# Attention of an adaptive-norm block in two groups of two batches, gates built on four partitions, output bias added by GpSimd

## What is computed

```python
mod = (_silu(L0_c) @ L0_wmod).reshape(L0_c.shape[0], 6, 1, -1)
sa, ca, ga, sb, cb, gb = (mod[:, 0], mod[:, 1], mod[:, 2], mod[:, 3], mod[:, 4], mod[:, 5])
ga = (2 * (ga >= 0) - 1) * jnp.maximum(jnp.abs(ga), 0.25)
gb = (2 * (gb >= 0) - 1) * jnp.maximum(jnp.abs(gb), 0.25)
h = _layernorm(x, axis=-1) * (1 + ca) + sa
x = x + ga * _L0_attn_ref(h, ...)
h = _layernorm(x, axis=-1) * (1 + cb) + sb
x = x + gb * _L0_ffn_ref(h, L0_ffn_w_gate, L0_ffn_w_up, L0_ffn_w_down)
```

## Time and profile before

| | us |
|---|---|
| median of 3 runs | 959.33 (958.27 to 960.14) |
| profiled execution | 958.83 |
| its span, first to last instruction | 957.1 |
| TensorE busy in the span | 663.8 (69%) |
| VectorE busy | 677.4 (71%) |
| GpSimd busy | 567.0 (59%) |
| ScalarE busy | 439.1 (46%) |

### The profile page before, as it was taken

One profiled execution on the slowest core, in us unless ns is written; L12 is line 12 of the kernel. 1 busy time (PEld: TensorE's weight loads), 2 busy tenths in 40 slices (PEclk: granted clock), 3 DMA queues, 4 the chain that ended last, 5 costly groups with the idle time before them and its releaser, 6 DMA issues.

```text
span 957.1 us, 8556 instructions
## 1 busy us (share of the span) xinstructions
PE 663.8 (69%) x2416; PEld 337.7 (35%) x2416; DVE 677.4 (71%) x867; ACT 439.1 (46%) x715; POOL 567.0 (59%) x297
## 2 busy tenths in 40 slices
PE   3675576567377797878788386787978744299990
PEld 2344244432032232323322032232323224288880
DVE  6742477566598889899945598999998865844430
ACT  2413142257576465555556666465565513022220
POOL 6101564400399888999900399898998913136555
PEclk9755677688589899899997589899999975599995
DMA  4000000000000000000000000000000061012222
GB/s 154 0 1 1 0 1 0 1 0 0 1 0 0 1 0 0 0 0 0 0 1 0 1 0 1 0 0 1 0 0 0 0 241 44 1 12 19 20 21 22
DMA packets 11363, 13.05 MB, mean 14 GB/s; under 512 B 1545, under 2 KB 9914, under 8 KB 10690
## 3 DMA queue, kind: packets, MB, share of 16 engines
q1 hardware_dynamic: 6434, 10.51, 3.0%
q0 software_dynamic: 4896, 2.13, 2.6%
HBM read 8.43 MB, written 4.21 MB: 13 GB/s over the span
## 4 chain that ended last, share of the span: by engine, by line
PE 33%; DVE 29%; issue 14%; POOL 10%; ACT 9%; DMA 2%; DVEq 1%; POOLq 0%; ACTq 0%; SPq 0%
PE ps L924 7%; DVE ps L1302 6%; DVE hs_all L1315 6%; POOL hc_all L456 4%; PE ps L1050 3%; PE ps L1066 3%; PE ps L1027 2%; DVE w_ffn L1315 2%; PE ps L930 2%; ACT ps L693 2%; PE ps L886 2%; PE ps L769 1%; POOL dbu L443 1%; DVE big L1117 1%; DVE dbu L1349 1%
## 5 line engine op out<-in xcount | busy, mean ns | idle before, releaser
L924 PE MATMUL ps<-hc_all,ident 128*128 128x512 f32 x512 | 264.0, 640 | 21.6 <-POOL hc_all L456 20.4
L456 POOL TENSOR_TENSOR hc_all<-hs_all,c_row 128x1024 f32<-128x1024 f32 x88 | 210.5, 2392 | 19.4 <-DVE hs_all L1315 16.2
L690 ACT COPY c_row<-ps 128x512 f32<-128x512 f32 x128 | 74.9, 585 | 161.6 <-PE ps L943 145.9
L924 PEld LDWEIGHTS ps<-hc_all,ident 128*128 128x128 f32 x512 | 100.5, 201 | 119.1 <-issue 73.6
L1315 DVE TENSOR_TENSOR_SCAN hs_all<-da,ps 128x1024 f32<-128x1024 f32 x48 | 109.8, 2287 | 11.6 <-ACT da L693 5.4
L693 ACT ACTIVATE da<-big,a_neg 128x511 f32 (+1 forms) x176 | 117.2, 716 | 0.0
L1302 DVE TENSOR_TENSOR ps<-big,ps 128x1024 f32<-128x1024 f32 x88 | 107.4, 1220 | 11.7 <-POOL big L432 4.8
L456 POOL TENSOR_TENSOR hc_all<-w_ffn,c_row 128x1024 f32<-128x1024 f32 x40 | 94.2, 2356 | 22.1 <-DVE w_ffn L1315 22.1
L1315 DVE TENSOR_TENSOR_SCAN hs_all<-ps,dbu 128x1024 f32<-128x1024 f32 x40 | 91.0, 2274 | 12.4 <-POOL hc_all L456 9.7
L443 POOL TENSOR_TENSOR dbu<-big,w_mod 128x1024 f32<-128x1024 f32 x40 | 96.1, 2401 | 0.0
L1315 DVE TENSOR_TENSOR_SCAN w_ffn<-da,ps 128x1024 f32<-128x1024 f32 x40 | 91.5, 2287 | 5.3
(11 more groups left out here) (253 smaller groups left out, 1103.3 us busy)
## 6 DMA issues: line engine op xcount, KB each, us to landing
tmpA<-w_in SPq DMA_DIRECT2D x2, 1024.0 KB, 6.9
tmpB<-w_in SPq DMA_DIRECT2D x2, 1024.0 KB, 9.0
x_tok<-x_in SPq DMA_DIRECT2D x1, 1024.0 KB, 6.6
out<-x_tok SPq DMA_DIRECT2D x1, 1024.0 KB, 7.2
xm_rows<-xn SPq DMA_DIRECT2D x1, 1024.0 KB, 5.3
w_mod<-w_mod_in SPq DMA_DIRECT2D x1, 768.0 KB, 4.6
out<-hc_all,hs_all POOLq DMA_INDIRECT x40, 3.0
w_ffn<-w_ffn_in SPq DMA_DIRECT2D x1, 560.0 KB, 7.4
```

The source lines that it names most:

```text
L456: nc.gpsimd.tensor_tensor(hc[:, n % 4, :, :], hs3[HS_BUF[n]].rearrange("p (i s) -> p i s", i=IC), c_row[:, n % 4, :].unsqueeze(1).to_broad ...
L690: nc.scalar.copy(c_row[:, n % 4, :], ps[:, CB, :]).then_inc(c_cs, 1)
L924: mm = nc.tensor.matmul(ps[:, YS + i, :], ident[:], hc[:, n % 4, i, :], start=(n == 0), stop=(n == NS - 1))
```

## The change

- Loads: x in two halves, `w_mod` by block, block 1's after `w_ffn`. The bias is loaded on 128 partitions (`bt_rows`).
- Modulation: block 0's shift and scale of the first norm stay columns (`modulation_cols`). All else is made as rows on four partitions, one per batch (`modulation_rows`: `silu_c` of four columns is the stationary side). ScalarE and VectorE make the gates there (`gate_rows`, `gate_signs`). Later a matmul with a broadcast column of the identity spreads a batch's row over 128 partitions (mod_bc). Block 1's are made after the attention.
- Attention: maxima, exps and sums in groups of two batches (`pool_max`, `key_weights`, `value_weights`). ScalarE copies the keys. The `w_ffn` rounding stands behind the key weights.
- Output: no matmul for the bias. GpSimd makes `bt_gate` and adds it to `x_tok`, four instructions of 128x512, and VectorE then adds the output of a batch and takes its statistics at once. `std` and `nmr` are made after every second batch. The transposes of `w_ffn` stand between batches 1 and 2, in banks 4 to 6.
- Some semaphores are merged, for block 1 too; its instructions and their order stay.

```diff
-            sp.dma_start(w_mod[:], w_mod_in).then_inc(ld_mod, 16)
-            sp.dma_start(x_tok[:], x_in).then_inc(ld_x, 16)
+            for k in range(2):
+                ts = slice(k * NT // 2, (k + 1) * NT // 2)
+                sp.dma_start(x_tok[:, ts, :], x_in[:, ts, :]).then_inc(ld_x[k], 16)
+                if k == 0:
+                    sp.dma_start(w_mod[:, 0, :], w_mod_in[:, 0, :]).then_inc(ld_mod[0], 16)
             sp.dma_start(w_attn[:], w_attn_in).then_inc(ld_attn, 16)
-            sp.dma_start(bt_row[:], bt_in).then_inc(ld_bt, 16)
             sp.dma_start(w_ffn[:], w_ffn_in).then_inc(ld_ffn, 16)
+            sp.dma_start(bt_rows[:], bt_in).then_inc(ld_bt, 16)
+            sp.dma_start(w_mod[:, 1, :], w_mod_in[:, 1, :]).then_inc(ld_mod[1], 16)
...
+            pool.wait_ge(ld_bt, 16)
+            pool.wait_ge(mod_done, 1)
+            chain.link(nc.gpsimd.tensor_tensor(bt_gate[:], bt_rows[:].unsqueeze(1).to_broadcast([P, B, D]), gates[:, 0, :, :],
+                                               ALU.mult))
+            for b in range(B):
+                pool.wait_ge(xn_ready, TB * (b + 1))
+                xb = x_tok[:, b * TB:(b + 1) * TB, :]
+                nc.gpsimd.tensor_tensor(xb, xb, bt_gate[:, b, :].unsqueeze(1).to_broadcast([P, TB, D]),
+                                        ALU.add).then_inc(x_bias, 1)
+            pool.wait_ge(mod_done, 2)
             modulate_x(0)
...
-            act.wait_ge(mod_raw, 3)
-            nc.scalar.activation(gate_abs, gates[:], ACT.Abs, scale=2.0).then_inc(mod_abs, 1)
...
+            def gate_rows(layer, rows, gate):
+                act.wait_ge(mod_mm, 2 + layer)
+                nc.scalar.copy(mod_rows[:, rows, :], ps[0:B, 7, 0:(4 - 2 * layer) * D].rearrange("p (j d) -> p j d", d=D))
+                nc.scalar.activation(row_abs[:, 2 * layer:2 * layer + 2, :],
...
+            def exps(k, g, at):
+                act.wait_ge(a_bias, 2 * k + g + 1)
+                for b in range(2 * g, 2 * g + 2):
+                    nc.scalar.activation(soft[:, b, :], ps[:, 4 + b, :], ACT.Exp, bias=sc4[:, at, b:b + 1], scale=SCALE,
+                                         accum_out=sc4[:, at + 1, b:b + 1]).then_inc(a_exp_s, 1)
+
...
+            keys(0)
+            keys(1)
+            exps(0, 0, 2)
+            keys(2)
+            keys(3)
+            exps(0, 1, 2)
             magnitudes(q_x, 0, w_ffn[:], q_mag[:])
...
+            act.wait_ge(mod_bc, 1)
+            nc.scalar.copy(gates[:, 0, :, :], ps[:, 0:B, 0:D]).then_inc(mod_done, 1)
+            act.wait_ge(a_pooled, B)
+            exps(1, 0, 9)
+            nc.scalar.copy(shift_b[:], ps[:, 0:B, D:2 * D])
+            nc.scalar.activation(scale_b[:], ps[:, 0:B, 2 * D:3 * D], ACT.Identity, bias=1.0)
+            nc.scalar.copy(gates[:, 1, :, :], ps[:, 0:B, 3 * D:4 * D]).then_inc(mod_done, 1)
+            exps(1, 1, 9)
...
+            def deviations(g):
+                ts = slice(g * NT // 2, (g + 1) * NT // 2)
+                act.wait_ge(stat_ready, NT + (g + 1) * NT // 2)
+                nc.scalar.activation(std[:, ts], mv[:, ts, 1], ACT.Sqrt, bias=eps[:, 0:1]).then_inc(std_ready, 1)
...
+            deviations(0)
             normalise_x(0)
             normalise_x(1)
+            deviations(1)
+            act.preload_act_table(ACT.Silu)
+            gate_rows(1, slice(4, 6), slice(0, 2))
             magnitudes(q_x, 1, x_flat(0), mag_x)
+            act.wait_ge(mod_bc, 2)
+            nc.scalar.copy(gates[:, 2:4, :, :].rearrange("p g (h k) d -> p h k g d", h=2),
+                           ps[:, 6:8, :].rearrange("p h (k g d) -> p h k g d", k=2, g=2)).then_inc(mod_done, 1)
...
-            def modulation():
-                pe.wait_ge(c_ready, 1)
-                pe.wait_ge(ld_mod, 16)
-
-                for b in range(B):
-                    nc.tensor.matmul(ps[:, b, :], silu_c[:, b:b + 1].to_broadcast([P, P]), w_mod[:, 0, 2 * D:6 * D],
-                                     start=True, stop=True).then_inc(mod_mm, 1)
-
-                for i, (layer, j) in enumerate([(0, 0), (0, 1), (1, 0), (1, 1), (1, 3), (1, 4)]):
-                    mm = nc.tensor.matmul(ps[:, 4, i * B:(i + 1) * B], w_mod[:, layer, j * D:(j + 1) * D],
+            def modulation_cols(layer, at, bank, first):
+                for i, j in enumerate(at):
+                    mm = nc.tensor.matmul(ps[:, bank, first + i * B:first + (i + 1) * B], w_mod[:, layer, j * D:(j + 1) * D],
                                           silu_c[:, layer * B:(layer + 1) * B], start=True, stop=True)
...
+            def modulation_rows(layer, first, cols):
+                return nc.tensor.matmul(ps[0:B, 7, first:first + cols.stop - cols.start], silu_c[:, layer * B:(layer + 1) * B],
+                                        w_mod[:, layer, cols], start=True, stop=True)
...
+            pe.wait_ge(c_ready, 1)
+            pe.wait_ge(ld_mod[0], 16)
+            modulation_cols(0, [0, 1], 4, 0).then_inc(mod_mm, 1)
+            pe.wait_ge(consts, 3)
+            transposes(0)
+            transposes(1)
+            modulation_rows(0, 0, slice(2 * D, 6 * D)).then_inc(mod_mm, 1)
+            transposes(2)
+            transposes(3)
+            pe.wait_ge(ld_attn, 16)
+            for b in range(B):
+                queries(b)
+            query_scores(0)
+            query_scores(1)
+            for b in range(2):
+                project(b, a_mk, w_attn[:, 2, :], hT[:, b * S:(b + 1) * S])
+            query_scores(2)
+            query_scores(3)
+            for b in range(2, B):
+                project(b, a_mk, w_attn[:, 2, :], hT[:, b * S:(b + 1) * S])
+            pe.wait_ge(mod_row, 1)
+            for b in range(B):
+                pe.wait_ge(a_mkT, b + 1)
+                mm = nc.tensor.matmul(ps[:, b, :], ident[0:B, b:b + 1].to_broadcast([B, P]),
+                                      mod_rows[:, 0:4, :].rearrange("p j d -> p (j d)"), start=True, stop=True)
+            mm.then_inc(mod_bc, 1)
             for b in range(B):
                 pe.wait_ge(a_pooled, b + 1)
                 pe.wait_ge(a_mkT, b + 1)
                 pe.wait_ge(a_exp_s, b + 1)
                 project(4 + b, a_score, wk_pooled[:, b, :], mkT[:, b * S:(b + 1) * S])
-            for b in range(B):
-                pe.wait_ge(a_pooled, B + b + 1)
-                for j in range(TB):
-                    nc.tensor.matmul(ps[:, b, j * P:(j + 1) * P], mqT[:, (b * TB + j) * P:(b * TB + j + 1) * P],
-                                     wt_pooled[:, b, :], start=True, stop=False)
-                    mm = nc.tensor.matmul(ps[:, b, j * P:(j + 1) * P], ones[0:1, :], bt_gate[:, b, :],
-                                          start=False, stop=True)
-                mm.then_inc(a_out, 1)
+            attended(0)
+            attended(1)
...
             pe.wait_ge(q_x["q_done"], 1)
-            pe.wait_ge(a_x, B)
+            pe.wait_ge(a_exp_s, 2 * B)
             for i in range(2):
                 for k, n in enumerate(KD):
-                    nc.tensor.transpose(ps[:, i, k * P:k * P + n], w_ffn[0:n, (3 * i + k) * D:(3 * i + k + 1) * D],
+                    nc.tensor.transpose(ps[:, 4 + i, k * P:k * P + n], w_ffn[0:n, (3 * i + k) * D:(3 * i + k + 1) * D],
                                         ident[0:n, 0:n])
             for k, n in enumerate(KD):
-                mm = nc.tensor.transpose(ps[0:n, 2, k * P:(k + 1) * P], w_ffn[:, 6 * D + k * P:6 * D + k * P + n], ident[:])
+                mm = nc.tensor.transpose(ps[0:n, 6, k * P:(k + 1) * P], w_ffn[:, 6 * D + k * P:6 * D + k * P + n], ident[:])
             mm.then_inc(f_wtr, 1)
+            attended(2)
+            attended(3)
+
+            pe.wait_ge(ld_mod[1], 16)
+            modulation_rows(1, 0, slice(2 * D, 3 * D))
+            modulation_rows(1, D, slice(5 * D, 6 * D))
+            modulation_cols(1, [0, 1, 3, 4], 7, 2 * D).then_inc(mod_mm, 1)
+            pe.wait_ge(mod_row, 2)
+            pe.wait_ge(mod_col, 2)
+            pe.wait_ge(f_wT, 3)
+            for b in range(B):
+                mm = nc.tensor.matmul(ps[:, 6 + b // 2, (b % 2) * 2 * D:(b % 2 + 1) * 2 * D], ident[0:B, b:b + 1].to_broadcast([B, P]),
+                                      mod_rows[:, 4:6, :].rearrange("p j d -> p (j d)"), start=True, stop=True)
+            mm.then_inc(mod_bc, 1)
...
+            def gate_signs(layer, rows):
+                dve.wait_ge(mod_raw, 1 + layer)
+                mine = slice(2 * layer, 2 * layer + 2)
+                chain.link(v.tensor_scalar(row_sign[:, mine, :], mod_rows[:, rows, :], 0.0, 0.5, ALU.is_ge, ALU.subtract))
+                v.scalar_tensor_tensor(mod_rows[:, rows, :], row_abs[:, mine, :], 2 * GATE_MIN, row_sign[:, mine, :],
+                                       ALU.max, ALU.mult).then_inc(mod_row, 1)
...
+            def value_weights(g):
+                pool_sum(1, g, mkT, 8)
+                mine = slice(2 * g, 2 * g + 2)
```

(31 more changed lines are left out.)

220 lines of the change are left out of this document (105 added, 115 removed).

## The result

The changed kernel takes 926.19 us (median of 4 runs, 923.15 to 927.67), the kernel before in the same runs 959.44 (958.27 to 960.14). The ratio is 0.9652, with a 95% interval from 0.9631 to 0.9674: some 33 us less. The profiled execution is the fastest of the four, 923.15 us, its span 921.4; the other three have spans of 925.6, 925.9 and 923.3.

What follows compares the result with a forecast made beforehand. Only the time to the first FFN block was at stake: VectorE busy first, then nothing full, then TensorE at half clock. Gains of 13.8 + 1.8 + 18.2 = 33.8 us from 958.83 gave 925.0 us; range 917 to 932.

Steps and rivals of the forecast that it cites:

- Part one: Up to `xn`: with split loads and gate work moved later, `xn` starts about 10.5 instead of 24.29, 13.8 us gained.
- Part two: From `xn` to the first output matmul: 34.7 us where it took 36.5, 1.8 us gained, 4.6 eaten by GpSimd.
- The contention: VectorE's `value_weights` and GpSimd's x additions alternate instead of running side by side: first weights at 45.2, not 40.6.
- Rival (c): Before the output, the maxima's bias operations also wait for GpSimd: weights 1.1 us later, 926.1 us; chance 0.08.
- Rival (b): Clock rises late at the start: four projections at 1.69 instead of 0.91 cost 3.1 us, 928 us; chance 0.17.
- Part three: From first output matmul to `scales_x(0)`: 16.4 us instead of 34.65, 18.2 us gained, 11.6 of it the sixteen L798.
- The tail by batches: Behind the output: additions, statistics and second norm overlap with the matmuls, the rest of 18.2 us beyond 11.6.
- Rival (e): Second norm doesn't go batch by batch, as `std` of group 0 comes late: 2 us more, 927 us; chance 0.07.
- At nothing: Items priced at zero, such as layer 1's rows, columns and broadcasts: about one us at most if broadcasts are late.
- Rival (d): Selective scan falls into a lower granted clock: slower than before, about 972 us at 0.78; chance 0.02.
- The drift: FFN and scan stages shift by clock phase: some 4 us allowed in the range; chance 0.06 of more either way.

## Why the prediction was right

The forecast was 925.0, measured was 926.19, and the range held it. The sum is right by more than its terms: up to `scales_x(0)` 33.8 us were forecast and 31.7 won, and two of its three parts were off by 3 us or more, with opposite signs.

- **Part one, up to `xn`.** The loads came near the slope that was drawn: first half of x in use at 6.37 (5.4 said), `w_mod` at 7.46 (6.3), second half at 8.72 (7.5), so `xn` starts at 11.57 for 10.5. What failed is a step that the prediction didn't name: it took `xn` at the 4.19 us of the earlier trace rows, where it had stood behind all of GpSimd's work. Moved 13 us forward it lies beside `row_sel`'s selects. Its end is won by 8.0 us (28.48 to 20.48), not by 13.8; the run with the selects held shows the cause. The Trainium skill ("SBUF — State Buffer", Who interferes with whom) has VectorE in a two-port mode, which `tensor_scalar` can take, and GpSimd exclude each other: whoever issues first keeps the shared pair for its whole instruction. By that rule, which the prediction used for the maxima only, `xn` had to wait for a select, and the trace agrees (one of the sixteen takes 3.85 us, a select 3.83).
- **Part two, to the output.** From the end of `xn` to the output it took 29.9 us (20.48 to 50.39), where the prediction had 30.5 (14.7 to 45.2). What the prediction worked out within it was there: the exposed load of the `Exp` table at 30.40, projections at the full clock (3.60 for four, from 22.62), the additions stretched beside the sums. The row matmul took 1.87, about twice what one of 512 columns takes from 22.62 on, as the cold start of the prediction had it, though the profile's rows give a granted clock of 1.00 there; the two don't fit, and no run explains it. The contention was forecast at 4.6; without the bias on GpSimd 3.0 were measured. Rival (c) was true in its mechanism, with bias operations of 1.15 and 1.12 us for 0.23, and 0.89 for a product, and came on top; but only one of the two sums was stretched. Rival (b), a late clock at the start, didn't come; the clock fell later instead, during the broadcasts, and cost nearly nothing, as the text had said of it.
- **Part three, from the output on.** Here the prediction had 16.4 us and it took 13.3. The wrong step is "a batch is 4 x 0.72 = 2.9 us, still at the low clock". In these runs a 128-row matmul costs 0.72 only where a one-row matmul stands next to it; alone it takes 0.47 cold, and as the clock rises, 0.27. So TensorE was never waited for, and the sixteen L798 were worth 14.2 us (27.5 less 13.3), not 11.6. In the kernel before they were worth more, 18.4 (34.65 less 16.2): there TensorE's own time for the output fell from 23.2 to 5.19, and the rest of the tail stood behind it. The tail by batches was sized nearly right: 6.6 by the prediction's own difference (18.2 less 11.6), 6.0 by experiment, 1.28 of it a table load that stood uncovered in that run alone. `std` of group 0 came behind the copies and a table load as said, and cost VectorE 1.15. Rival (e) didn't come.
- **At nothing.** Block 1's broadcasts (3.77 us at 66.80) end at 70.57, and TensorE's first transposes of x stand at 70.50, 0.7 behind the end of GpSimd's rescale (68.73 to 69.79). That is 6.8 us behind `scales_x(0)` for 6.0 in before, and the second `scales_x` follows the first by 13.64 us for 13.53. So this item cost no more than the one us that the text allowed.
- **Behind it.** Rival (d), a slower scan, didn't come. The drift that was allowed, 4 us either way, is there and has a size: some 3 us in the Mamba layers (585.9 to 589.8), and some 3 us in the FFN stage (97.4 to 100.6 from `scales_x(0)` to the third norm's `std`).

The sign was safe: its largest term was sixteen matmuls that stood alone on the path in the earlier trace rows. The number was close because errors cancelled. With the length of `xn` seen and the output mis-sized it would have been 5.8 us higher, with the output sized right and `xn` missed 3.1 lower. And the sum itself was 2.1 too large (33.8 for 31.7); that the median came within 1.2 of the forecast is in part the doing of stages that it left at nothing, in which this profile won 3.9.

## What to carry to other kernels

When an instruction moves forward in time, look up what each engine that shares its ports does there, not only where it stood: an edit that saves a wait can put a cheap instruction beside a long GpSimd one. Read the cost of a matmul from a row in which its neighbours are the same as in the kernel to be predicted; a one-row matmul made its 128-row neighbours half as dear again and kept the clock low, and filling its rows with zeros took both back. And an edit of one us isn't told by a median here: date it at the first instruction that both programs share, and look at the clock in the window ahead before giving it a cause.

## What the runs showed that was not expected

- Few rows cost more than many. Sixteen pairs with a one-row matmul took 0.72 us a matmul, at the lower of the two clocks (1.2 GHz) for 23.2 us of unbroken work; with 128 rows 0.43, and the clock rose to the full 2.4 GHz before the second batch was done. Four-row broadcasts of 512 columns, without a gap, ended in a fall from 0.97 to 0.50; with 128 rows it stayed at 1.00.
- A `tensor_scalar` of 128x2, two numbers a partition, takes 0.23 us alone and up to 1.35 beside GpSimd's `tensor_tensor`; sixteen of 128x128 took 8.91 us for 4.19 beside `affine_select`. `tensor_reduce` wasn't stretched: out of PSUM it kept its 0.69 beside `tensor_tensor`, and one of 128x1120 out of SBUF took 1.32 beside the held `affine_select` (15.93 in that run), 1.31 without it.
- Contention moves on. With `xn` free 4.5 us were won at the transposes and 2.5 at the output; two scale operations of 0.20 took 2.76 and 3.31 beside the held selects; with one bias operation taken out, the first sum went from 0.68 to 1.80. Only the versions without GpSimd's additions got rid of it for the sums.
